# A two-layer transformer decoder on one Trainium2 core: the cross-attention softmax handed on by four heads instead of eight

## The chip, the core and the metric

The kernel runs on one core of one Trainium2 chip. A core has five engines, each with its own instruction queue that is worked off strictly in order: TensorE (PE in the profile, with its weight loads as PEld), VectorE (DVE), ScalarE (ACT), GpSimd (POOL) and SyncE (SP, which here only issues transfers). They meet through semaphores. The metric is device time in microseconds of one execution. Three executions of the kernel before took 549.65, 549.88 and 549.92 us, median 549.88 us.

## The reference, cut to what matters

Sixteen sequences of 128 tokens with 128 features pass through six residual blocks, each behind a layer norm:

```python
x = x + attn0(ln(x))            # self0: 16 heads of 8, causal
x = x + xattn0(ln(x), ctx)      # cross0: 8 heads of 64
x = x + ternary_ffn(ln(x))      # ffn
x = x + attn1(ln(x))            # self1: 16 heads of 8, causal, scores clipped
x = x + xattn1(ln(x), ctx)      # cross1: 16 heads of 64
x = x + mixture(ln(x))          # moe: 8 experts, gated
```

The part at issue is the softmax of the two cross attentions. For each head, with 128 queries on the partitions and 128 keys along the row:

```python
attn = softmax(scores, axis=-1)   # max, exp(scores - max), sum, division
out  = attn @ v
```

## The kernel before

The program is a stream of small steps. A step has a name such as `cross1.rc.1` (stage, step, chunk), and each exists once per sequence. A chunk is eight heads (`UNIT` = 8), so that one chunk's scores are a tile of 128 x 1024 float32 in one of two PSUM groups `S`. cross0 has one chunk per sequence and cross1 two, which makes 3 x 16 = 48 chunks of cross softmax. In this text `@7` behind a step's name is the sequence.

What one chunk of cross softmax does, step by step:

- `s1` (PE, `cross_scores1`, line 986; matmuls at L995): eight score tiles into a group of S.
- `mx` (DVE, `negative_max`, L769): one reduction over 128 x 1024 to eight negated maxima.
- `ex` (ACT, `cross_exps`, L649): eight exponentials of 128 x 128, from S to `diff` (also called `e`) in SBUF. The last one frees the group of S.
- `rc` (DVE, `reciprocal_sums`, L776 to L778): one reduction over 128 x 1024 to eight sums, a drain, eight reciprocals.
- `nz` (POOL, `divide_by_sum`, L577): one multiplication over 128 x 1024, in place.
- `t` (PE, `turn_over`, L1008): eight transposes into a group of S.
- `wT` (ACT, `weights_by_key`, L658) copies them to SBUF, and `pv` (PE, L1035) multiplies with the values.

self0 also has a `t` step, with the same helper and line; its input is made by `self0.mx` on DVE (`less_max`, L785 and L787: maximum, drain, subtraction, each over 128 x 1024, for two chunks per sequence). Its transposes are named `diff_self` in the trace, those of the cross stages `diff_cross`.

The order of all steps on each engine is settled before the program is written. The class `Plan` (line 199) places steps by estimated weights and by the priorities in the table `FORWARD`, and runs up to a dozen sequences in different stages beside each other. `run` (line 483) then writes each engine's steps out in that order. So an engine that waits at one step holds back all that is behind it. A step's waits and semaphore counts are written out in its helper, and the two groups of S and the four banks X are shared by all stages in the planned turn.

Of the kernel before, what the change touches and what calls it, by code (L numbers as in the profile page):

```python
# [9 lines left out]
ALU = mybir.AluOpType  # L10
ACT = mybir.ActivationFunctionType
AX_X = mybir.AxisListType.X

P = 128
# [3 lines left out]
UNIT = 8  # L18
# [16 lines left out]
class Step:  # L35
# [280 lines left out]
class CrossAttention(Attention):  # L316
    def __init__(self, nc, ctx, name, heads):
        Attention.__init__(self, nc, ctx, name, heads, heads // UNIT, XD, heads // UNIT, True)
        self.v = [self.sb(f"v{b}", [P, heads, XD]) for b in range(AHEAD[name])]
        self.kT = [self.sb(f"kT{b}", [P, heads // 2, P]) for b in range(AHEAD[name])]  # L320
        self.qT = self.sb("qT", [P, heads // 2, P])
        self.e = self.diff
        self.e_sum = self.sb("e_sum", [P, self.units, UNIT])
        self.e_rec = self.sb("e_rec", [P, self.units, UNIT])
        self.max_ready = [self.sem(f"max_ready{u}") for u in range(self.units)]
        self.rec_ready = [self.sem(f"rec_ready{u}") for u in range(self.units)]


def halves(ap):
# [4 lines left out]
def v_halves(v):  # L334

    return v[:].rearrange("p h s w -> p (h s w)").bitcast(BF16).rearrange(
        "p (h s w two) -> p h s w two", s=3, w=SD + 1, two=2)[:, :, :, :, 1]


def place(head):  # L340

    return 4 * (head % 2) + head % UNIT // 2


def decoder(nc, t, out):
    ctx = ExitStack()
    with ctx:
# [3 lines left out]
        def sem(name):  # L351
            return ctx.enter_context(nc.semaphore(name))
# [4 lines left out]
        x_full, s_full = sem("x_full"), sem("s_full")  # L357
# [13 lines left out]
        def score(i, *names):  # L371

            return max(scored[i, n] for n in names)
# [54 lines left out]
        self0 = SelfAttention(nc, ctx, "self0", True)  # L428
# [83 lines left out]
        def _(pool):  # L512
# [60 lines left out]
                    .then_inc(L.low_ready[u], 1)  # L573

            def divide_by_sum(L, i, u):
                pool.wait_ge(L.rec_ready[u], i + 1)
                pool.tensor_tensor(L.diff[u][:].rearrange("p (h k) -> p h k", h=UNIT),  # L577
                                   L.e[u][:].rearrange("p (h k) -> p h k", h=UNIT),
                                   L.e_rec[:, u, :].unsqueeze(2).broadcast_to([P, UNIT, P]), ALU.mult)\
                    .then_inc(L.diff_ready[u], 1)  # L580

            def mix_experts(i):
                pool.wait_ge(*taken(i, "moe.e"))
# [27 lines left out]
        def _(act):  # L611
# [29 lines left out]
            def cross_exps(L, i, u):  # L641

                turn = f"{L.name}.s1.{u}"
                S_ = group(i, turn)
                act.wait_ge(L.max_ready[u], i + 1)
                if i:
                    act.wait_ge(s_full, score(i - 1, f"{L.name}.t.{u}"))
                for p in range(UNIT):
                    last = act.activation(L.e[u][:, P * p:P * (p + 1)], S_[:, P * p:P * (p + 1)], ACT.Exp,  # L649
                                          bias=L.row_max[:, u, p:p + 1])  # L650
                last.then_inc(taken(i, turn)[0], 1)

            def weights_by_key(L, i, u):
# [19 lines left out]
            def do_step(i, name, L, step, u):  # L673
# [39 lines left out]
                if step == "ex" and L in (cross0, cross1):  # L713
                    cross_exps(L, i, u)
# [24 lines left out]
        def _(dve):  # L739
# [26 lines left out]
            def negative_max(L, i, u):  # L766
                turn = f"{L.name}.s1.{u}"
                dve.wait_ge(s_full, score(i, turn))
                dve.tensor_reduce(L.row_max[:, u, :], group(i, turn)[:].rearrange("p (h k) -> p h k", h=UNIT), AX_X,  # L769
                                  ALU.max, negate=True).then_inc(L.max_ready[u], 1)  # L770

            def reciprocal_sums(L, i, u):
                dve.wait_ge(*taken(i, f"{L.name}.s1.{u}"))
                if i:
                    dve.wait_ge(L.diff_ready[u], i)
                dve.tensor_reduce(L.e_sum[:, u, :], L.e[u][:].rearrange("p (h k) -> p h k", h=UNIT), AX_X, ALU.add)  # L776
                dve.drain()
                dve.reciprocal(L.e_rec[:, u, :], L.e_sum[:, u, :]).then_inc(L.rec_ready[u], 1)  # L778

            def less_max(L, i, u):  # L780
                scores = group(i, f"{L.name}.s1", u)[:].rearrange("p (h k) -> p h k", h=UNIT)
# [111 lines left out]
            def do_step(i, name, L, step, u):  # L893
# [44 lines left out]
        def _(pe):  # L938
# [5 lines left out]
            def room_for_scores(i, name, turns=1):  # L944
                for k in range(turns):
                    if plan.turn[i, name, k][0]:
                        pe.wait_ge(s_free[plan.bank[i, name, k]], plan.turn[i, name, k][0])
# [38 lines left out]
            def cross_scores1(L, i, name, c):  # L986
                pe.wait_ge(*emptied(i, f"{L.name}.q.{c}"))
                pe.wait_ge(*emptied(i, f"{L.name}.k.{c}"))
                if i:
                    pe.wait_ge(L.diff_ready[c], i)  # L990
                room_for_scores(i, name)
                S_, kT = group(i, name), L.kT[i % AHEAD[L.name]]
                for h in range(UNIT * c, UNIT * (c + 1)):
                    rows, at = slice(XD * (h % 2), XD * (h % 2 + 1)), P * place(h)
                    last = pe.matmul(S_[:, at:at + P], L.qT[rows, h // 2, :],  # L995
                                     kT[rows, h // 2, :],
                                     start=True, stop=True)
                last.then_inc(s_full, 1)

            def turn_over(L, i, name, u):  # L1000
                if L is self0:
                    S_ = group(i, f"{L.name}.s1", u)
                else:
                    S_ = group(i, name)
                    room_for_scores(i, name)
                pe.wait_ge(L.diff_ready[u], i + 1)
                for k in range(UNIT):
                    last = pe.transpose(S_[:, P * k:P * (k + 1)], L.diff[u][:, P * k:P * (k + 1)], ident[:])  # L1008
                last.then_inc(s_full, 1)

# [199 lines left out]
```

## Time and profile before

| | |
|---|---|
| median of three executions | 549.88 us |
| the profiled execution itself | 549.28 us |
| span of its trace | 547.5 us |
| PE / ACT / DVE / POOL busy | 516.0 / 436.6 / 400.7 / 383.2 us |
| instructions | 15960 |

The span goes from the first to the last instruction of the program; the execution's own time also holds 1.8 us around it. Busy time of an engine is the time in which at least one of its instructions was at work. Matmuls overlap one another and their ends are modelled, so for PE the starts of matmuls say more than the busy time.

### The profile page before, as it was taken

The page shows a single profiled execution, that of the slowest core. Times are in us where ns is not written, and L with a number is a line of the kernel's source. Part 1 is how long each engine was busy: PE and PEld are TensorE (multiplying, and loading weights), DVE is VectorE, ACT ScalarE, POOL GpSimd, SP SyncE. Part 2 cuts the span into 40 slices and gives each one's busy share as a digit, 9 for nine tenths or more (in the row PEclk, how much of TensorE's full clock was granted, in tenths as well). Part 3 has the DMA queues.
Part 4 walks back from the last instruction along what each step waited for, and adds up shares of the span by engine and source line. Part 5 has one row for each costly group of instructions (what it writes and reads, how often), then busy time and mean ns, then how long its engine had stood idle before and what let it go on. Part 6 is the DMA issues. An engine that isn't in the chain of part 4 may idle for free.

```text
span 547.5 us, 15960 instructions
## 1 busy us (share of the span) xinstructions
PE 516.0 (94%) x5506; PEld 414.3 (76%) x5506; DVE 400.7 (73%) x904; ACT 436.6 (80%) x1154; POOL 383.2 (70%) x566
## 2 busy tenths in 40 slices
PE   4999979899999999999999999999999999999974
PEld 3778657687788888887887978878788877777851
DVE  1655857786879798888878797978887758665553
ACT  3678775889789897998888888989888886898641
POOL 5356547877687879787778788776886756575454
PEclk9999998999999999999999999999999999999987
DMA  6800000000000000000000000000000000000000
GB/s 198 306 2 2 1 1 2 1 3 2 2 1 8 2 7 3 6 2 8 2 6 2 8 1 2 7 2 8 1 7 1 2 6 8 1 6 2 7 6 10
DMA packets 6462, 8.95 MB, mean 16 GB/s; under 512 B 1008, under 2 KB 4848, under 8 KB 6384
## 3 DMA queue, kind: packets, MB, share of 16 engines
q1 hardware_dynamic: 6384, 7.94, 4.4%
q8 instruction: 45, 0.74, 0.6%
q14 instruction: 33, 0.27, 0.2%
HBM read 6.50 MB, written 1.05 MB: 14 GB/s over the span
## 4 chain that ended last, share of the span: by engine, by line
PE 72%; issue 7%; POOL 6%; ACT 5%; POOLq 5%; DVE 4%; DVEq 2%; ACTq 0%
PE X L952 14%; PE S L1008 10%; PE S L995 8%; PE X L1044 8%; PE X L1035 7%; PE X L1092 6%; PE S L982 5%; PE S L1128 3%; POOL w_low_self L572 3%; ACT diff_cross L649 3%; PE X L1055 2%; PE X L1146 2%; PE X L1021 2%; POOL diff_cross L577 2%; POOLq L544 1%
## 5 line engine op out<-in xcount | busy, mean ns | idle before, releaser
L572 POOL TENSOR_TENSOR w_low_self<-w_self 128x1024 f16<-128x1024 f32 x64 | 120.5, 1893 | 47.8 <-ACT w_self L638 32.0
L649 ACT ACTIVATE diff_cross<-S,row_max_cross 128x128 f32<-128x128 f32 x384 | 103.7, 408 | 5.3 <-DVE row_max_cross L769 5.1
L577 POOL TENSOR_TENSOR diff_cross<-diff_cross,e_rec_cross 128x1024 f32<-128x1024 f32 x48 | 91.0, 1897 | 17.4 <-DVE e_rec_cross L778 17.2
L769 DVE TENSOR_REDUCE row_max_cross<-S 128x8 f32<-128x1024 f32 x48 | 58.4, 1218 | 28.7 <-PE S L995 28.6
L776 DVE TENSOR_REDUCE e_sum_cross<-diff_cross 128x8 f32<-128x1024 f32 x48 | 58.3, 1215 | 9.9 <-ACT diff_cross L649 9.9
L658 ACT ACTIVATE w_cross<-S 128x1024 f32<-128x1024 f32 x48 | 50.0, 1048 | 6.5 <-PE S L1008 6.1
L1008 PE MATMUL S<-ident,diff_cross 128*128 128x128 f32 x384 | 49.7, 274 | 5.2 <-POOL diff_cross L577 3.1
L995 PE MATMUL S<-kT_cross,qT_cross 64*128 64x128 f32 x768 | 52.6, 281 | 2.2 <-ACT qT_cross L614 1.1
L1008 PEld LDWEIGHTS S<-ident,diff_cross 128*128 128x128 f32 x384 | 42.9, 141 | 12.8 <-issue 4.4
L796 DVE SCALAR_TENSOR_TENSOR w_self<-S,s_bound 128x1024 f32<-128x1024 f32 x32 | 37.6, 1216 | 19.2 <-PE S L982 19.2
L995 PEld LDWEIGHTS S<-kT_cross,qT_cross 64*128 64x128 f32 x768 | 45.7, 187 | 7.7 <-issue 4.5
L1035 PEld LDWEIGHTS X<-w_cross,v_cross 128*64 128x64 f32 x768 | 41.6, 138 | 13.0 <-issue 7.4
L1035 PE MATMUL X<-w_cross,v_cross 128*64 128x128 f32 x768 | 51.1, 279 | 0.2 <-issue 0.2
L614 ACT ACTIVATE attnT_cross<-X 128x512 f32<-128x512 f32 x48 | 28.7, 601 | 22.1 <-PE X L1035 21.7
L785 DVE TENSOR_REDUCE row_max_self<-S 128x8 f32<-128x1024 f32 x32 | 38.9, 1217 | 3.7 <-PE S L982 3.6
L787 DVE TENSOR_TENSOR diff_self<-S,row_max_self 128x1024 f32<-128x1024 f32 x32 | 39.2, 1225 | 2.4
L982 PE MATMUL S<-by_head_self,plain_self 32*128 32x512 f32 x256 | 37.8, 661 | 1.4 <-ACT diff_cross L649 1.3
L638 ACT ACTIVATE w_self<-S 128x1024 f32<-128x1024 f32 x32 | 33.2, 1036 | 6.6 <-PE S L1008 6.6
L614 ACT ACTIVATE qT_cross<-X 128x512 f32<-128x512 f32 x48 | 28.7, 599 | 11.2 <-PE X L952 11.1
L614 ACT ACTIVATE by_head_self<-X,head_mask 128x128 f32<-128x128 f32 x128 | 36.4, 378 | 0.0
L614 ACT ACTIVATE kT_cross<-X 128x512 f32<-128x512 f32 x48 | 29.8, 622 | 7.6 <-PE X L952 7.6
L1008 PE MATMUL S<-ident,diff_self 128*128 128x128 f32 x256 | 33.7, 275 | 1.9 <-DVE diff_self L787 1.7
(156 smaller groups left out, 1299.1 us busy)
## 6 DMA issues: line engine op xcount, KB each, us to landing
out_dram<-x_all SPq DMA_DIRECT2D x16, 64.0 KB, 1.5
x_all<-in_x SPq DMA_DIRECT2D x1, 768.0 KB, 6.9
cT_all<-in_ctx SPq DMA_DIRECT2D x1, 768.0 KB, 8.8
e_k<-in_e_k SPq DMA_DIRECT2D x1, 512.0 KB, 4.5
e_v<-in_e_v SPq DMA_DIRECT2D x1, 512.0 KB, 5.5
e_q<-in_e_q SPq DMA_DIRECT2D x1, 512.0 KB, 8.6
e_o<-in_e_o SPq DMA_DIRECT2D x1, 512.0 KB, 10.5
m_w<-in_m_w SPq DMA_DIRECT2D x1, 512.0 KB, 8.8
```

Source lines behind the costliest of these rows:

```text
L572: pool.tensor_tensor(L.w_low[u][:], L.w[u][:], halves(L.w[u][:]), ALU.subtract)\
L577: pool.tensor_tensor(L.diff[u][:].rearrange("p (h k) -> p h k", h=UNIT), L.e[u][:].rearrange("p (h k) -> p h k", h=UNIT), L.e_rec[:, u, :] ...
L614: act.activation(dst, src, ACT.Copy, **scale).then_inc(emptied(i, name)[0], 1)
L649: last = act.activation(L.e[u][:, P * p:P * (p + 1)], S_[:, P * p:P * (p + 1)], ACT.Exp, bias=L.row_max[:, u, p:p + 1])
L658: act.activation(L.w[u][:], group(i, turn)[:], ACT.Copy).then_inc(taken(i, turn)[0], 1)
L769: dve.tensor_reduce(L.row_max[:, u, :], group(i, turn)[:].rearrange("p (h k) -> p h k", h=UNIT), AX_X, ALU.max, negate=True).then_inc(L.ma ...
L776: dve.tensor_reduce(L.e_sum[:, u, :], L.e[u][:].rearrange("p (h k) -> p h k", h=UNIT), AX_X, ALU.add)
L952: last = pe.matmul(bank(i, name)[:, P * k:P * (k + 1)], w[:, col:col + P], xT, start=True, stop=True)
L982: last = pe.matmul(group(i, name, u)[:, 512 * half:512 * (half + 1)], L.plain[rows, :], L.by_head[rows, :, :].rearrange("p j n -> p (j n)" ...
L995: last = pe.matmul(S_[:, at:at + P], L.qT[rows, h // 2, :], kT[rows, h // 2, :], start=True, stop=True)
L1008: last = pe.transpose(S_[:, P * k:P * (k + 1)], L.diff[u][:, P * k:P * (k + 1)], ident[:])
L1035: last = pe.matmul(bank(i, name)[rows, P * pair:P * (pair + 1)], v[:, h, :], L.w[c][:, P * place(h):P * (place(h) + 1)], start=True, stop= ...
```

## The change

The planned steps, their order and their weights stay as they are. Inside the steps `mx`, `ex`, `rc` and `nz` of the cross stages, each chunk is worked in two pieces of four heads, and each piece is announced by itself. `row_max`, `e_sum`, `e_rec` and `e` are the same tensors. The semaphores `max_ready`, `rec_ready` and `diff_ready` of the cross stages now count two per chunk and sequence, and a new one, `exp_half`, is raised by the fourth exponential. The group of S is still freed by the eighth. The transposes of a cross chunk wait for the first piece before the first and for the second before the fifth.

```diff
+def pieces(i):
+    return [(slice(0, 4), 1), (slice(4, 8), 1)]
+
+def columns(ap, heads):
+    return ap[:, P * heads.start:P * heads.stop].rearrange("p (h k) -> p h k", k=P)
...
             def divide_by_sum(L, i, u):
-                pool.wait_ge(L.rec_ready[u], i + 1)
-                pool.tensor_tensor(L.diff[u][:]..., L.e[u][:]..., L.e_rec[:, u, :]..., ALU.mult)\
-                    .then_inc(L.diff_ready[u], 1)
+                for heads, n in pieces(i):
+                    pool.wait_ge(L.rec_ready[u], 2 * i + heads.stop // 4)
+                    pool.tensor_tensor(columns(L.diff[u], heads), columns(L.e[u], heads), ..., ALU.mult)\
+                        .then_inc(L.diff_ready[u], n)
...
             def cross_exps(L, i, u):
-                act.wait_ge(L.max_ready[u], i + 1)
-                if i:
-                    act.wait_ge(s_full, score(i - 1, f"{L.name}.t.{u}"))
-                for p in range(UNIT):
-                    last = act.activation(L.e[u][:, P * p:P * (p + 1)], ...)
+                for heads, n in pieces(i):
+                    act.wait_ge(L.max_ready[u], 2 * i + heads.stop // 4)
+                    if i and heads.start == 0:
+                        act.wait_ge(s_full, score(i - 1, f"{L.name}.t.{u}"))
+                    for p in range(heads.start, heads.stop):
+                        last = act.activation(L.e[u][:, P * p:P * (p + 1)], ...)
+                    if heads.stop == 4:
+                        last.then_inc(L.exp_half[u], 1)
                 last.then_inc(taken(i, turn)[0], 1)
...
             def negative_max(L, i, u):
                 dve.wait_ge(s_full, score(i, turn))
-                dve.tensor_reduce(L.row_max[:, u, :], ..., ALU.max, negate=True).then_inc(L.max_ready[u], 1)
+                for heads, n in pieces(i):
+                    dve.tensor_reduce(L.row_max[:, u, heads], columns(group(i, turn), heads), ...)\
+                        .then_inc(L.max_ready[u], n)
...
             def reciprocal_sums(L, i, u):
-                dve.wait_ge(*taken(i, f"{L.name}.s1.{u}"))
-                ...
-                dve.tensor_reduce(L.e_sum[:, u, :], ..., ALU.add)
-                dve.drain()
-                dve.reciprocal(L.e_rec[:, u, :], L.e_sum[:, u, :]).then_inc(L.rec_ready[u], 1)
+                for heads, n in pieces(i):
+                    if heads.stop == 4:
+                        dve.wait_ge(L.exp_half[u], i + 1)
+                    else:
+                        dve.wait_ge(*taken(i, f"{L.name}.s1.{u}"))
+                    if i and heads.start == 0:
+                        dve.wait_ge(L.diff_ready[u], 2 * i)
+                    dve.tensor_reduce(L.e_sum[:, u, heads], columns(L.e[u], heads), AX_X, ALU.add)
+                    dve.drain()
+                    dve.reciprocal(L.e_rec[:, u, heads], L.e_sum[:, u, heads]).then_inc(L.rec_ready[u], n)
...
             def turn_over(L, i, name, u):
                 if L is self0:
                     S_ = group(i, f"{L.name}.s1", u)
+                    pe.wait_ge(L.diff_ready[u], i + 1)
                 else:
                     S_ = group(i, name)
                     room_for_scores(i, name)
-                pe.wait_ge(L.diff_ready[u], i + 1)
                 for k in range(UNIT):
+                    if L is not self0 and (k == 4 or k == 0):
+                        pe.wait_ge(L.diff_ready[u], 2 * i + 1 + k // 4)
                     last = pe.transpose(S_[:, P * k:P * (k + 1)], L.diff[u][:, P * k:P * (k + 1)], ident[:])
```

## Rows read from the trace of the kernel before

**Rows 1.** Windows: busy us (instructions) of PE, PEld, DVE, ACT, POOL; clock; DMA.

```profile
20.00:150.00 130.00, 121.30 (x1305) 94.87 (x1304) 90.94 (x188) 102.06 (x262) 83.41 (x122) 0.99 0.05 16
150.00:440.00 290.00, 289.40 (x3272) 238.80 (x3272) 237.71 (x532) 253.02 (x676) 229.00 (x322) 1.00 0.02 4
440.00:547.50 107.50, 92.85 (x848) 71.16 (x846) 63.84 (x168) 71.50 (x193) 61.95 (x88) 0.96 0.02 5
```

**Rows 2.** Groups: line, tiles, count | busy us, mean ns | idle before us, its releaser.

```profile
L649 ACT ACTIVATE diff_cross<-S,row_max_cross 128x128 f32<-128x128 f32 x384 | 103.7, 408 | 5.3 <-DVE row_max_cross L769 5.1
L577 POOL TENSOR_TENSOR diff_cross<-diff_cross,e_rec_cross 128x1024 f32<-128x1024 f32 x48 | 91.0, 1897 | 17.4 <-DVE e_rec_cross L778 17.2
L776 DVE TENSOR_REDUCE e_sum_cross<-diff_cross 128x8 f32<-128x1024 f32 x48 | 58.3, 1215 | 9.9 <-ACT diff_cross L649 9.9
L1008 PE MATMUL S<-ident,diff_cross 128*128 128x128 f32 x384 | 49.7, 274 | 5.2 <-POOL diff_cross L577 3.1 <-ACT w_cross L658 1.1 <-ACT diff_cross L649 0.7
```

**Rows 3.** Groups with shorter rows of the same kinds of instruction, same columns.

```profile
L808 DVE TENSOR_REDUCE o_sum_self<-X 128x144 f32<-128x432 f32 x32 | 19.2, 600 | 4.4 <-PE X L1023 4.4
L586 POOL TENSOR_TENSOR weighted<-weighted 128x512 f32<-128x512 f32 x16 | 20.3, 1269 | 6.6 <-DVE weighted L865 6.6
L588 POOL TENSOR_TENSOR weighted<-weighted 128x256 f32<-128x256 f32 x16 | 11.6, 728 | 2.3
```

**Rows 4.** Timeline of DVE: start, us, what, [idle before, releaser].

```profile
312.81 0.29 DVE L828 TENSOR_TENSOR x_all<-X,x_all 128x128 f32<-128x128 f32 x1 [0.21 <-PE X L1044]
...
315.36 1.22 DVE L776 TENSOR_REDUCE e_sum_cross<-diff_cross 128x8 f32<-128x1024 f32 x1
...
321.70 1.23 DVE L787 TENSOR_TENSOR diff_self<-S,row_max_self 128x1024 f32<-128x1024 f32 x1
...
325.37 1.21 DVE L769 TENSOR_REDUCE row_max_cross<-S 128x8 f32<-128x1024 f32 x1
326.50 0.15 DVE L843 RECIPROCAL g_rec<-g_sum 128x1 f32<-128x1 f32 x1
```

**Rows 5.** Timeline of PE in the same stretch (sequence 12), same columns.

```profile
322.98 1.09 PE L1008 MATMUL S<-ident,diff_self 128*128 128x128 f32 x8
```

**Rows 6.** Timeline, DVE and PE: the same pair in sequences 7 and 14.

```profile
174.34 1.23 DVE L787 TENSOR_TENSOR diff_self<-S,row_max_self 128x1024 f32<-128x1024 f32 x1
175.62 1.09 PE L1008 MATMUL S<-ident,diff_self 128*128 128x128 f32 x8
...
382.01 1.23 DVE L787 TENSOR_TENSOR diff_self<-S,row_max_self 128x1024 f32<-128x1024 f32 x1
383.29 0.33 PE L1008 MATMUL S<-ident,diff_self 128*128 128x128 f32 x1
```

**Rows 7.** Timelines of DVE and PE: sequence 13, with two sums ahead of it.

```profile
346.38 1.21 DVE L776 TENSOR_REDUCE e_sum_cross<-diff_cross 128x8 f32<-128x1024 f32 x1
347.79 1.20 DVE L776 TENSOR_REDUCE e_sum_cross<-diff_cross 128x8 f32<-128x1024 f32 x1
...
353.02 1.22 DVE L787 TENSOR_TENSOR diff_self<-S,row_max_self 128x1024 f32<-128x1024 f32 x1
354.49 0.38 PE L1008 MATMUL S<-ident,diff_self 128*128 128x128 f32 x2
```

**Rows 8.** Timelines: where PE waits for the cross softmax (start, sequences 2 and 14).

```profile
42.33 0.44 PE L967 MATMUL S<-mask,ident_b 32*32 32x512 bf16 x16 [0.39 <-ACT diff_cross L649]
80.17 1.90 POOL L577 TENSOR_TENSOR diff_cross<-diff_cross,e_rec_cross 128x1024 f32<-128x1024 f32 x1
82.22 0.95 PE L1008 MATMUL S<-ident,diff_cross 128*128 128x128 f32 x7 [1.73 <-POOL diff_cross L577]
503.10 1.21 DVE L776 TENSOR_REDUCE e_sum_cross<-diff_cross 128x8 f32<-128x1024 f32 x1
504.67 1.90 POOL L577 TENSOR_TENSOR diff_cross<-diff_cross,e_rec_cross 128x1024 f32<-128x1024 f32 x1 [5.30 <-DVE e_rec_cross L778]
506.71 0.96 PE L1008 MATMUL S<-ident,diff_cross 128*128 128x128 f32 x7 [0.85 <-POOL diff_cross L577]
```

More of the change, by code:

```diff
@@ L326, in __init__ @@
         self.rec_ready = [self.sem(f"rec_ready{u}") for u in range(self.units)]
+        self.exp_half = [self.sem(f"exp_half{u}") for u in range(self.units)]
 def halves(ap):
@@ L575, in divide_by_sum @@
             def divide_by_sum(L, i, u):
-                pool.wait_ge(L.rec_ready[u], i + 1)
-                pool.tensor_tensor(L.diff[u][:].rearrange("p (h k) -> p h k", h=UNIT),
-                                   L.e[u][:].rearrange("p (h k) -> p h k", h=UNIT),
-                                   L.e_rec[:, u, :].unsqueeze(2).broadcast_to([P, UNIT, P]), ALU.mult)\
-                    .then_inc(L.diff_ready[u], 1)
+                for heads, n in pieces(i):
+                    pool.wait_ge(L.rec_ready[u], 2 * i + heads.stop // 4)
+                    pool.tensor_tensor(columns(L.diff[u], heads), columns(L.e[u], heads),
+                                       L.e_rec[:, u, heads].unsqueeze(2).broadcast_to([P, 4 * n, P]), ALU.mult)\
+                        .then_inc(L.diff_ready[u], n)
             def mix_experts(i):
@@ L644, in cross_exps @@
                 S_ = group(i, turn)
-                act.wait_ge(L.max_ready[u], i + 1)
-                if i:
-                    act.wait_ge(s_full, score(i - 1, f"{L.name}.t.{u}"))
-                for p in range(UNIT):
-                    last = act.activation(L.e[u][:, P * p:P * (p + 1)], S_[:, P * p:P * (p + 1)], ACT.Exp,
-                                          bias=L.row_max[:, u, p:p + 1])
+                for heads, n in pieces(i):
[3 more added lines that the diff above has]
+                    for p in range(heads.start, heads.stop):
+                        last = act.activation(L.e[u][:, P * p:P * (p + 1)], S_[:, P * p:P * (p + 1)], ACT.Exp,
+                                              bias=L.row_max[:, u, p:p + 1])
+                    if heads.stop == 4:
+                        last.then_inc(L.exp_half[u], 1)
                 last.then_inc(taken(i, turn)[0], 1)
@@ L768, in negative_max @@
                 dve.wait_ge(s_full, score(i, turn))
-                dve.tensor_reduce(L.row_max[:, u, :], group(i, turn)[:].rearrange("p (h k) -> p h k", h=UNIT), AX_X,
-                                  ALU.max, negate=True).then_inc(L.max_ready[u], 1)
+                for heads, n in pieces(i):
+                    dve.tensor_reduce(L.row_max[:, u, heads], columns(group(i, turn), heads), AX_X,
+                                      ALU.max, negate=True).then_inc(L.max_ready[u], n)
             def reciprocal_sums(L, i, u):
-                dve.wait_ge(*taken(i, f"{L.name}.s1.{u}"))
-                if i:
-                    dve.wait_ge(L.diff_ready[u], i)
-                dve.tensor_reduce(L.e_sum[:, u, :], L.e[u][:].rearrange("p (h k) -> p h k", h=UNIT), AX_X, ALU.add)
-                dve.drain()
-                dve.reciprocal(L.e_rec[:, u, :], L.e_sum[:, u, :]).then_inc(L.rec_ready[u], 1)
+                for heads, n in pieces(i):
[8 more added lines that the diff above has]
+                    dve.reciprocal(L.e_rec[:, u, heads], L.e_sum[:, u, heads]).then_inc(L.rec_ready[u], n)
             def less_max(L, i, u):
@@ L989, in cross_scores1 @@
                 if i:
-                    pe.wait_ge(L.diff_ready[c], i)
+                    pe.wait_ge(L.diff_ready[c], 2 * i)
                 room_for_scores(i, name)
```

## Prediction

> **What bounds the kernel now.** I first read the busy time of each engine by stretch [rows 1]. From 150 to 440 us PE is busy 289.40 of 290.00 us, with DVE at 82%, ACT at 87% and POOL at 79%: in the middle PE bounds, and nearly every delay put into PE's queue lengthens the kernel by as much. Up to 150 us PE sits idle for 8.70 of 130 us and after 440 us for 14.65 of 107.5 us; there, chains of waits matter and a shorter softmax could pay.
>
> Next come the groups, for what each engine of the cross softmax waits for before its step [rows 2]. The reader is to see how little idle time the softmax's own latency causes. ACT is idle before its 384 exponentials for 5.3 us in all. PE is idle before the 384 cross transposes for 3.1 us because of POOL. The plan puts `t` late enough that the chain of mx, ex, rc and nz is long finished in the middle.
>
> Then the timeline, for what PE does wait for in the middle. DVE works without a pause from 312.81 us, released by PE's `cross1.y`, until well past 326 us, and on this run stand in this order: three residuals, `cross1.rc.1`, `self1.at`, `self0.mx.0`, `self0.mx.1` [rows 4]. The last subtraction ends at 321.70 + 1.23 = 322.93 us, and PE's `self0.t.1` starts at 322.98 [rows 5]: it is just in time, with 0.05 us for the semaphore. The first and the last sequence with this pattern show the same 0.05 us: 175.57 to 175.62 and 383.24 to 383.29 us [rows 6]. Six sequences have it with one cross sum ahead in the run (7, 8, 9, 10, 12, 14). So the resource with no slack is DVE's run ahead of self0's transposes, and the change makes just that run longer.
>
> **The change part by part.**
>
> *DVE, maxima.* A reduction over 1024 occupies DVE from 325.37 to 326.50, 1.13 us [rows 4]. The slope comes from 432 against 1024 elements: (1.215 - 0.600) / 592 = 1.04 ns each, 1.064 us for 1024 [rows 2, 3]. Two halves cost one fixed part more: 1.13 - 1.06 = 0.07 us. The upper bound is the whole fixed part of the duration, 1.215 - 1.064 = 0.15 us, if the halves did not overlap.
>
> *DVE, sums.* A step `rc` takes 1.41 us start to start, 346.38 to 347.79 [rows 7]. Split, its reduction's fixed part, the drain and the reciprocals come twice: 1.41 - 1.06 = 0.35 us more. Lower bound: 0.12 us, should the second reduction hide all but the reciprocals' issue. Upper bound: 0.50 us, with the 0.15 us above for a wait between the halves. I take 0.35, since nothing after a drain overlaps in these rows. Where the step now waits for `ex` (9.9 us of idle in all, [rows 2]), the first half is hidden in that wait and `rc` ends about 0.5 us earlier instead. In sum 48 x (0.07 + 0.35) = 20 us of DVE work.
>
> The next instruction starts at 326.50, 0.08 us before the reduction ends at 325.37 + 1.21 = 326.58 [rows 4]. The Trainium skill, "VectorE: DVE Perf Modes", section "The DRAIN you can't avoid", says that the next operation does not start before the pipe is empty; by that rule the split maxima would cost the upper 0.15 us and each run below 0.1 to 0.2 us more. The trace does not bear it out.
>
> *POOL.* From 512 and 256 elements, 1.269 and 0.728 us, a slope of 2.11 ns and a fixed part of 0.19 us [rows 3]. A half of the division is then (1.897 - 0.19) / 2 + 0.19 = 1.04 us, the pair 0.19 us longer (bounds 0, if fixed parts overlap, and 0.19); 48 x 0.19 = 9 us. In the middle POOL has 61 of 290 us idle [rows 1], three divisions per sequence of 29 us make 0.6 us, and no step of PE there is released by POOL within that: I take nothing.
>
> *ACT.* The exponentials stay as they are, with one more wait and increment in their midst: between 0 and 48 x 0.05 us (the semaphore's time above) = 2.4 us; I take 0, as ACT would only stop there if DVE's second half were late, and that takes 0.7 us against four exponentials of 103.7 / 384 = 0.27 us each [rows 2], 1.1 us. Starting earlier pays only where ACT is idle before the first one: 5.1 us, mostly at the start [rows 2].
>
> *PE.* No instruction more; one more wait in the middle of each cross `t`. When PE arrives the semaphore is mostly set; bounds 0 and 48 x 0.05 = 2.4 us, and I take 0.
>
> *What PE loses in the middle.* Each sum ahead of `self0.t.1` in an unbroken run delays it by 0.35 us. Split maxima ahead of `cross1.res` are covered by the 0.21 us of idle before 312.81 [rows 4]. Six sequences x 0.35 = 2.1 us. Sequences 6 and 13 have both chunks' sums and maxima in the run, 2 x 0.42 = 0.84 us; 13 has 354.49 - 354.24 = 0.25 us in hand, of which the semaphore takes 0.05 [rows 7], so it loses 0.64, and 6, which is tight, 0.8. Sequences 11 and 15 have looser ends; I put 0.3 and 0.2 us. Sum 4.0 us. Behind PE stand all later steps, and DVE's run starts from PE's `cross1.y` again, so these delays add up over the sequences and aren't made good; a tenth I let go for waits on other engines: 3.6 us.
>
> *What PE gains at the ends.* At 42.33 PE waits 0.39 us for the group of S that `cross0.ex.0@0` frees, and ACT stood idle before it: 0.4 us. At 82.22 it waited 1.73 us for POOL; that division starts at 80.17 with no idle time before it, so POOL came from other work and had its sums already [rows 8]; two halves end 0.2 us later than one, and only the transposes of the first half move up: 0.2 us. In sequence 14 sum, division and transposes follow each other directly [rows 8]: the first division can start at 503.10 + 0.7 + 0.3 = 504.1 instead of 504.67, the second ends at 506.2 to 506.4, and only four transposes are then left: 0.5 us; sequence 13 has 0.2 us in the same way. Sum 1.3 us. The last sequence's end is made by the experts' steps, which don't change.
>
> **The sum.** The profiled execution took 549.28 us: 549.28 + 3.6 - 1.3 = 551.6 us. That execution was 0.6 us under the median of the three runs, 549.88; moved there, 552.2 us, 0.4% slower.
>
> **The rivals.**
>
> *The delays are swallowed.* PE isn't quite full: 0.60 us of idle in the middle by these windows, and starts that lie further apart than they need. If PE's delay at `self0.t.1` only replaces waits it would have had later for ACT, the loss falls to about 1.3 us and the ends pay it back. For it: ACT and DVE are both above 80%. Against: the run is released by PE itself. Time: 549.9 us.
>
> *The shorter chain wins, on the other side.* Place: the transposes of the cross stages, and the start of the exponentials. Per chunk the time from scores to transposes shrinks by half a reduction twice (1.1 us) and half a division (0.9 us), less the fixed parts. Price: the 3.1 us of PE's waits before cross transposes plus the 0.4 us at the start go [rows 2, 8], and DVE's 20 us find room in the 290 - 237.7 = 52 us it has idle in the middle. It decides if the added 0.35 us is less than what the run gains at its head, that is if `rc` stands where DVE waits. For it: POOL idles 17.2 us on the reciprocals. Against: these are the ends, and before `self0.mx` DVE has no pause. Time: 549.9 - 3.5 = 546.4 us. The Trainium skill, "Perfetto Trace Analysis", section "Optimizing Scalar/DVE Operations", gives a rule for this side: where an unsaturated engine makes bubbles on another, cutting its instructions up can finish work sooner. In this trace the bubbles are few.
>
> *The small delays breed.* The upper prices (0.50 + 0.15 us per chunk) make each run 0.6 us longer, and further steps with little in hand behind them (the experts' weights, `cross1.t.1`) come late too: 4.0 x 0.6 / 0.35 = 6.9 us, less 1.3 and with 1 us for those steps, 556.5 us.
>
> **How the numbers follow.** Forecast 0.46, swallowed 0.24, shorter chain 0.17, breeding 0.13. The time is the forecast's, 552.2 us; its own range is 551.0 to 554.0. For 8 in 10 the range takes in the swallowed case whole and part of the other two: 548.8 to 556.0. A difference of under 0.2% (1.1 us) is about what can't be told from no change. Slower by more: forecast and breeding, 0.59; within: 0.24; faster: 0.17.
>
> **What would show it.** In the profile after, DVE should be busy some 20 us more, and reductions over 512 should take about 0.68 us each; POOL some 8 us more. The timeline should show `self0.t.1` of sequences 7 to 14 starting 0.05 us after a later DVE, with PE idle before it and DVE named as its releaser, and PE's idle in the middle up by 2 to 4 us. Before the cross transposes POOL's name should shrink below 3.1 us. I am wrong if a split `rc` costs under 0.2 us, if DVE's run ahead of `self0.mx` starts earlier relative to PE, or if the ends gain more than 3 us.

## The result: 0.26% slower, and the profile after

Median 550.67 us for the changed kernel beside 549.49 us for the kernel before in the same comparison: ratio 1.0026, 95% interval 1.0016 to 1.0035, which is 0.9 to 1.9 us more. The prediction said 552.2 us and "slower by more than 0.2%" with 0.59. Its sign holds. Its time is 1.5 us too high: 0.4 us of that is the kernel before, which came out at 549.49 us here instead of 549.88, and the rest is the size of the change, forecast at 2.3 us and measured at 1.4 us by the ratio (1.2 us by the medians). That the change is past 0.2% (1.1 us) hangs on the point value; the interval begins at 0.9 us. The profiled execution took 550.7 us with a span of 549.0 us and 16200 instructions.

Windows of the kernel after; columns as in [rows 1], which they answer:

```profile
20.00:150.00 130.00, 121.61 (x1295) 94.83 (x1294) 92.69 (x212) 101.23 (x261) 83.78 (x130) 0.97 0.05 17
150.00:440.00 290.00, 288.85 (x3250) 236.88 (x3247) 244.04 (x620) 251.56 (x671) 231.57 (x349) 1.00 0.02 4
440.00:549.00 109.00, 94.59 (x880) 73.04 (x878) 67.69 (x200) 74.04 (x199) 65.08 (x101) 0.98 0.02 6
```

PE stays full in the middle; DVE is busy there for 6.3 us more than before (244.04 against 237.71). Groups of the page after, to set beside [rows 2]: line, tiles, count, then busy and mean, then idle before and releaser.

```profile
L660 ACT ACTIVATE diff_cross<-S,row_max_cross 128x128 f32<-128x128 f32 x384 | 103.7, 410 | 2.8 <-DVE row_max_cross L783 2.6
L588 POOL TENSOR_TENSOR diff_cross<-diff_cross,e_rec_cross 128x512 f32<-128x512 f32 x96 | 97.7, 1039 | 8.8 <-DVE e_rec_cross L796 8.8
L783 DVE TENSOR_REDUCE row_max_cross<-S 128x4 f32<-128x512 f32 x96 | 61.4, 682 | 28.5 <-PE S L1013 28.4
L794 DVE TENSOR_REDUCE e_sum_cross<-diff_cross 128x4 f32<-128x512 f32 x96 | 64.2, 669 | 2.9 <-ACT diff_cross L660 2.2 <-issue 0.3
...
L1028 PE MATMUL S<-ident,diff_cross 128*128 128x128 f32 x384 | 50.0, 274 | 3.8 <-ACT diff_cross L660 1.2 <-POOL diff_cross L588 1.2 <-ACT w_cross L671 1.1
...
L1028 PE MATMUL S<-ident,diff_self 128*128 128x128 f32 x256 | 34.2, 277 | 2.7 <-DVE diff_self L805 2.3
```

Everything that a shorter chain should shorten did get shorter: ACT's idle time before the exponentials fell from 5.3 to 2.8 us, POOL's before the divisions from 17.4 to 8.8, DVE's before the sums from 9.9 to 2.9, PE's on POOL from 3.1 to 1.2 us. The kernel is slower all the same. What pays for it is in DVE's run; here is the run of sequence 12 in the trace after, the counterpart of [rows 4, 5] (start, us, what, and in brackets the idle time before, which is printed from 0.15 us on):

```profile
314.70 0.29 DVE L846 TENSOR_TENSOR x_all<-X,x_all 128x128 f32<-128x128 f32 x1
...
317.25 0.69 DVE L794 TENSOR_REDUCE e_sum_cross<-diff_cross 128x4 f32<-128x512 f32 x1
318.00 0.18 DVE L796 RECIPROCAL e_rec_cross<-e_sum_cross 128x4 f32<-128x4 f32 x1
318.10 0.65 DVE L794 TENSOR_REDUCE e_sum_cross<-diff_cross 128x4 f32<-128x512 f32 x1
318.83 0.18 DVE L796 RECIPROCAL e_rec_cross<-e_sum_cross 128x4 f32<-128x4 f32 x1
318.93 0.61 DVE L826 TENSOR_REDUCE o_sum_self<-X 128x144 f32<-128x432 f32 x1
...
323.87 1.23 DVE L805 TENSOR_TENSOR diff_self<-S,row_max_self 128x1024 f32<-128x1024 f32 x1
```

The run is released by PE as before. In both traces the residual starts 0.31 us after the last matmul of `cross1.y` (312.50 and 314.39 us); DVE is idle ahead of it for 0.21 us before and 0.14 us after, since the chunk's split maxima ahead of it take 0.07 us of that. PE in the same stretch:

```profile
322.08 0.61 PE L1075 MATMUL X<-xnT_self,d_qk 128*128 128x128 f32 x4
322.72 1.09 PE L1028 MATMUL S<-ident,diff_self 128*128 128x128 f32 x8
...
324.65 0.61 PE L1075 MATMUL X<-xnT_self,a_qk 128*128 128x128 f32 x4
325.15 1.09 PE L1028 MATMUL S<-ident,diff_self 128*128 128x128 f32 x8
```

The sum takes 318.93 - 317.25 = 1.68 us now. From the residual that PE's `cross1.y` releases to `self0.t.1` it is 325.15 - 314.70 = 10.45 us, where [rows 4, 5] have 322.98 - 312.81 = 10.17. That is 0.28 us more, and PE still starts 325.15 - (323.87 + 1.23) = 0.05 us behind DVE. The transposes have no idle bracket: PE's wait hides in the modelled end of the matmul before. Starts show it. Here are the same two PE instructions ahead of `self0.t.0` in the kernel before:

```profile
320.19 0.61 PE L1055 MATMUL X<-xnT_self,d_qk 128*128 128x128 f32 x4
320.64 1.04 PE L1008 MATMUL S<-ident,diff_self 128*128 128x128 f32 x8
```

0.45 us from start to start before, 0.64 after, and the group's mean rose from 275 to 277 ns instead of its idle time.

So from here on I read each trace by starts of PE's steps against those of the kernel before. All kernels have the same 5506 matmuls in the same order, so they can be set side by side one by one. The table's "middle" is how much such a shift grows between `cross1.y` of sequence 0 (134.5 us before) and of sequence 10 (430.0 us); at 1.00 granted clock in all of them. "Clock" is the granted clock in the windows 80 to 90 and 520 to 530 us.

| kernel | time against before, us (95%) | middle, us | clock 80:90, 520:530 |
|---|---|---|---|
| before | | | 0.83, 0.83 |
| after | +1.4 (0.9 to 1.9) | +2.57 | 0.67, 1.00 |
| after, once more | +1.4 (0.4 to 2.4) | +2.64 | 0.66, 0.83 |
| only sums split | +2.7 (1.9 to 3.6) | +3.19 | 0.67, 0.86 |
| only division split | -0.5 (-1.5 to 0.4) | +0.22 | 0.83, 0.83 |
| only maxima split | -1.0 (-1.8 to -0.2) | -0.60 | 0.83, 0.83 |
| all split, only at the ends | -1.8 (-2.7 to -0.8) | -0.14 | 0.66, 1.00 |
| all split, 13 sums in the run whole | -1.7 (-2.6 to -0.8) | +0.11 | 0.83, 0.83 |
| dose in the run, 0.285 us x 10 | +1.9 (0.9 to 2.9) | +2.15 | 0.66, 0.83 |
| same dose off the run | -0.4 (-1.3 to 0.5) | 0.00 | 0.73, 1.00 |
| double dose in the run, 0.611 us x 10 | +5.3 (4.2 to 6.3) | +5.12 | 0.72, 0.91 |
| ends, and maxima everywhere | -1.4 (-2.5 to -0.3) | -0.22 | 0.83, 0.83 |
| 13 sums whole, division at the ends | -1.3 (-2.5 to 0.0) | +0.06 | 0.66, 0.83 |

The times are the ratios of each comparison times 549.9 us. A ratio is not the quotient of the two medians: the medians differ by 3.4 us for "only sums split", 2.0 for "after, once more", 0.0 for "only division split" and +0.3 for "same dose off the run". All of these lie in their intervals, so single tenths of a microsecond in this column mean nothing.

### The profile page after: what moved, and what is told of

Read it like the earlier page. It is cut to its first block, busy times and chain, and to the rows that moved or that the text cites. A ratio compares the mean times of both kernels' runs of the same rounds, so it can differ in the third digit from the quotient of the medians.

```text
span 549.0 us, 16200 instructions
## 1 busy us (share of the span) xinstructions
PE 517.5 (94%) x5506; PEld 414.3 (75%) x5506; DVE 412.5 (75%) x1048; ACT 437.2 (80%) x1154; POOL 389.7 (71%) x614
## 4 chain that ended last, share of the span: by engine, by line
PE 71%; DVE 6%; issue 6%; ACT 5%; POOLq 4%; POOL 4%; DVEq 4%; ACTq 0%
PE X L970 13%; PE S L1028 10%; PE S L1013 8%; PE X L1055 7%; PE X L1064 7%; PE X L1112 6%; PE S L1000 4%; PE S L1148 4%; ACT diff_cross L660 3%; POOL w_low_self L582 2%; PE X L1075 2%; PE X L1166 2%; DVEq L804 2%; PE X L1041 2%; POOLq L554 1%
## 5 line engine op out<-in xcount | busy, mean ns | idle before, releaser
L588 POOL TENSOR_TENSOR diff_cross<-diff_cross,e_rec_cross 128x512 f32<-128x512 f32 x96 | 97.7, 1039 | 8.8 <-DVE e_rec_cross L796 8.8
L783 DVE TENSOR_REDUCE row_max_cross<-S 128x4 f32<-128x512 f32 x96 | 61.4, 682 | 28.5 <-PE S L1013 28.4
L794 DVE TENSOR_REDUCE e_sum_cross<-diff_cross 128x4 f32<-128x512 f32 x96 | 64.2, 669 | 2.9 <-ACT diff_cross L660 2.2
L642 ACT ACTIVATE w_self<-w_self,shift 128x1024 f32<-128x1024 f32 x32 | 35.5, 1140 | 0.0
```

The costliest lines, as they stand in the source:

```text
L588: pool.tensor_tensor(columns(L.diff[u], heads), columns(L.e[u], heads), L.e_rec[:, u, heads].unsqueeze(2).broadcast_to([P, 4 * n, P]), ALU ...
L783: dve.tensor_reduce(L.row_max[:, u, heads], columns(group(i, turn), heads), AX_X, ALU.max, negate=True).then_inc(L.max_ready[u], n)
L794: dve.tensor_reduce(L.e_sum[:, u, heads], columns(L.e[u], heads), AX_X, ALU.add)
```

## The experiments

All kernels come from the changed one by three switches, which say for each stage, sequence and chunk whether a part is split; with all three on it is the changed kernel, with all off the kernel before.

```diff
-def pieces(i):
-    return [(slice(0, 4), 1), (slice(4, 8), 1)]
+HALVES = [slice(0, 4), slice(4, 8)]
+def parts(split, L, i, u):     # split is max_split, sum_split or div_split
+    return HALVES if split(L.name, i, u) else [slice(0, 8)]
...
-                for heads, n in pieces(i):
+                for heads in parts(sum_split, L, i, u):
```

**Which part of the change costs.** Only the sums:

```diff
 def max_split(L, i, u):
-    return True
+    return False
 def div_split(L, i, u):
-    return True
+    return False
```

> Only the sums and reciprocals are split, all sixteen sequences; maxima and division are whole, and the division waits for both halves. Theory: self0.t loses 0.3 us in each of the sequences 7 to 14, 2.5 to 3 us in all as with the whole change, and little is gained at the ends since the division is not handed on: 551.5 to 552.5 us. Rival 1 (the loss comes from the maxima or from POOL's halves): 549.5 us, self0.t unmoved. Rival 2 (the second half's latency is hidden in the pipe and the loss is PE's additional waits): 549.5 to 550 us.

Measured: +2.7 us (median 553.31 us), so at or above the top of what I expected. It looks worse than the whole change, but the intervals overlap. Sequence 12 in its trace:

```profile
315.10 0.29 DVE L871 TENSOR_TENSOR x_all<-X,x_all 128x128 f32<-128x128 f32 x1 [0.21 <-PE X L1090]
...
317.01 0.18 DVE L783 BATCH_NORM_AGGREGATE mean_var_cross<-moments_cross 128x2 f32<-128x6 f32 x1 [0.42 <-issue]
...
317.99 0.69 DVE L819 TENSOR_REDUCE e_sum_cross<-diff_cross 128x4 f32<-128x512 f32 x1
...
324.62 1.23 DVE L830 TENSOR_TENSOR diff_self<-S,row_max_self 128x1024 f32<-128x1024 f32 x1
```

```profile
323.47 1.09 PE L1054 MATMUL S<-ident,diff_self 128*128 128x128 f32 x8 [0.17 <-DVE diff_self L830]
325.90 1.09 PE L1054 MATMUL S<-ident,diff_self 128*128 128x128 f32 x8
```

The run is again released by PE's `cross1.y` with 0.21 us of idle, as in [rows 4], and PE follows its end by 0.05 us. The split sums alone make a loss in the middle as large as that of the whole change. That it is 3.19 us and not 2.6 has another cause. From residual to `self0.t.1` it is 325.90 - 315.10 = 10.80 us here, 0.35 more than the 10.45 above, and the row at 317.01 shows why: DVE stands still for 0.42 us and waits for nothing that the profile shows. Such stops are in every trace and fall on other instructions when DVE's queue holds more or fewer of them (see the last section). In this trace sequences 9 and 12 lose 0.61 and 0.69 us, where each has one split sum of 0.27 us.

Only the division (`div_split` true, the others false):

> Only the division on POOL is split, with the transposes' waits; sums and maxima are whole. Theory: DVE's run ahead of self0.mx is as before, so no loss in the middle; the first four transposes of a chunk can start 1 us after the division's start at the ends: 548.5 to 549.3 us. Rival 1 (POOL's added 6.5 us of work or PE's added waits cost in the middle, up to 48 x 0.05 us): 550 to 552 us. Rival 2 (nothing at the ends comes from the division): 549.5 us.

Measured: -0.5 us, an interval that holds zero. My range of 548.5 to 549.3 us was missed by the median (549.93), and the second rival (nothing gained at the ends) fits as well. POOL's longer pairs and PE's added waits cost nothing that can be told. Only the maxima:

> Only the maxima are split, in all sixteen sequences; sums and division are whole. Theory: 0.07 us per chunk more for DVE, most of it hidden at the head of the run by cross1.res's wait for PE, and the exponentials can start 0.5 us earlier where ACT waits: 549 to 550 us, no difference that can be told. Rival 1 (any added instruction in DVE's queue costs): 0.6 us x 10 sequences of run and a start 0.15 us later each, 551.5 us. Rival 2 (the ends' gain of 1.8 us comes from the exponentials' earlier start): 548 us.

Measured: -1.0 us, 0.2 to 1.8 faster, which lies between the theory and its second rival: part of the ends' gain is the exponentials' earlier start. The 0.46 us at PE's group of S at 42.33 [rows 8] is gained. The middle gives 0.60 us, but 0.38 of it comes in one step, in sequence 10, and no wait of the softmax goes away there. In the kernel before, one of DVE's stops falls into that sequence's run; with the maxima split it falls elsewhere. First the kernel before, then the one with split maxima:

```profile
257.18 0.60 DVE L808 TENSOR_REDUCE o_sum_self<-X 128x144 f32<-128x432 f32 x1
258.22 0.26 DVE L812 RECIPROCAL X<-o_sum_self 128x16 f32<-128x16 f32 x1 [0.44 <-issue]
```

```profile
257.01 0.59 DVE L851 TENSOR_REDUCE o_sum_self<-X 128x144 f32<-128x432 f32 x1
257.68 0.26 DVE L855 RECIPROCAL X<-o_sum_self 128x16 f32<-128x16 f32 x1
```

The three parts add up within the noise: in the middle 3.19 + 0.22 - 0.60 = 2.81 beside 2.57 and 2.64 for the whole; in time 2.7 - 0.5 - 1.0 = 1.2 beside 1.4 us. As the stops fall differently in each, that they agree to 0.2 us is partly luck.

**Where it costs.** Everything split, but 13 of 48 sums left whole, those in the run:

```diff
 def sum_split(L, i, u):
-    return True
+    return not (L == "cross1" and u == 1 and 1 <= i <= 10) and not (L == "cross1" and i in (1, 8, 10))
```

> Everything is split but the sums that stand in DVE's run ahead of self0.mx: cross1's second chunk of sequences 1 to 10 and its first of 1, 8 and 10 have whole sums (13 of 48). Their maxima and divisions are still split. Theory: the loss of self0.t in sequences 6 to 15 falls from about 3 us to under 0.6 us, the ends' gain stays: 547.8 to 548.8 us, faster than both kernels. Rival (any added DVE work costs, wherever it stands): 35 of 48 sums still split, 550.4 us. Rival (the split maxima ahead in the run cost as well): 549.5 to 550 us.

Measured: -1.7 us, and the middle shifts by 0.11 us instead of 2.6. The median, 548.48 us, lies in the range expected. With 35 of 48 sums still split, the loss is gone. In its trace, sequence 12:

```profile
314.52 1.22 DVE L819 TENSOR_REDUCE e_sum_cross<-diff_cross 128x8 f32<-128x1024 f32 x1
...
320.87 1.23 DVE L830 TENSOR_TENSOR diff_self<-S,row_max_self 128x1024 f32<-128x1024 f32 x1
...
322.85 0.69 DVE L819 TENSOR_REDUCE e_sum_cross<-diff_cross 128x4 f32<-128x512 f32 x1
```

The sum ahead of `self0.mx` is whole, the one behind it is split. Splitting only at the two ends:

```diff
 def sum_split(L, i, u):          # max_split and div_split alike
-    return True
+    return (i <= 2 or i >= 12) if L == "cross0" else (i == 0 or i >= 11)
```

> Maxima, sums and division are split only at the two ends: cross0 of sequences 0 to 2 and 12 to 15, cross1 of sequences 0 and 11 to 15; all other chunks run as before the change. Theory (the middle loses because a split sum is 0.3 us longer ahead of self0.mx in DVE's unbroken run, the ends gain): the middle is as before, the ends keep what they gave, 0.6 us without the granted clock and up to 1.8 us with it, so 547.7 to 548.9 us. Rival 1 (any added DVE work costs): a third of the split chunks costs a third of 1.2 us, 549.9 us. Rival 2 (the gain at the end was the granted clock alone and not the change): 549.3 to 549.7 us, with self0.t of sequences 7 to 12 where they were before.

Measured: -1.8 us, 548.1 us, as expected, so the ends gain by themselves. The second rival, that this gain is granted clock, is answered by the executions with the same mean clock. At 0.989 this kernel has a median of 548.10 us (8 executions) and the kernel before 549.69 (14 in the same comparison), 1.6 us more; the kernel that spares the run has 548.59 us (8). In the second comparison of the changed kernel ("once more") it has 551.29 us at 0.989 and the kernel before 549.93 (8 each), so its loss isn't clock either.

**Is it DVE's time, and nothing of the hand-over?** The kernel before, with work that nobody uses (and one fill of `idle_in` on POOL at the start):

```diff
                     dve.reciprocal(L.e_rec[:, u, heads], L.e_sum[:, u, heads]).then_inc(L.rec_ready[u], 1)
+                if L.name == "cross1" and u == 1 and 1 <= i <= 10:
+                    dve.tensor_reduce(idle_out[:], idle_in[:].rearrange("p (a b) -> p a b", a=2), AX_X, ALU.max)
```

> The kernel before, with one idle reduction over 2x128 numbers (about 0.33 us of DVE, its result used by nobody) right behind the reciprocals of cross1's second chunk in sequences 1 to 10, so ten of them ahead of self0.mx of sequences 6 to 15. Nothing is split. Theory: each delays self0.t by its own duration, so 0.2 to 0.33 us in each sequence, 2.3 to 3.3 us in all, 552 to 553 us. Rival (the loss comes of the hand-over in halves, its waits and latencies, and not of DVE's time): 549.5 to 550 us.

Measured: +1.9 us. That is under the 2.3 to 3.3 us expected; of this range the interval (0.9 to 2.9) holds the lower part. One dose, in its timeline of DVE:

```profile
315.91 0.29 DVE L876 TENSOR_TENSOR x_all<-X,x_all 128x128 f32<-128x128 f32 x1 [0.20 <-PE X L1095]
...
319.75 0.20 DVE L824 RECIPROCAL e_rec_cross<-e_sum_cross 128x8 f32<-128x8 f32 x1
319.87 0.37 DVE L826 TENSOR_REDUCE idle_out<-idle_in 128x2 f32<-128x256 f32 x1
...
325.08 1.23 DVE L835 TENSOR_TENSOR diff_self<-S,row_max_self 128x1024 f32<-128x1024 f32 x1
```

```profile
326.37 1.09 PE L1059 MATMUL S<-ident,diff_self 128*128 128x128 f32 x8
```

The row says 0.37 us, but it overlaps its neighbours: by start to start it takes 0.285 us, and the stretch from residual to `self0.t.1` is 326.37 - 315.91 = 10.46 us, the same 10.45 as with the split sum. Ten doses of 0.285 put in 2.85 us, and 2.15 us come out in the middle, with no hand-over split. The sequences 13 and 15 pass on nothing, as their runs have something in hand; the other eight pass on 2.15 of 2.28 us. The same dose elsewhere (`L.name == "cross0" and 3 <= i <= 12`):

> The kernel before, with the same idle reduction, ten of them, behind the reciprocals of cross0's one chunk in sequences 3 to 12, which stands outside the run ahead of self0.mx but for sequences 13 and 15. Nothing is split. Theory: DVE has idle time there (52 of 290 us in the middle), so 549.5 to 550.2 us. Rival (any DVE time costs, wherever it stands): the same 552 to 553 us as with the reductions behind cross1's sums.

Measured: -0.4 us, an interval that holds zero, and a middle of 0.00 us. Two of the ten doses lie ahead of the measured stretch, at 102 and 129 us; nine of the ten have a wait of DVE of 0.65 us or more behind them before the next `self0` subtraction, which takes them up. The same DVE work costs 1.9 us in one place and nothing that can be told in the other. And twice the dose in the run (a second such line):

> The kernel before, with two of the idle reductions at each of the ten places behind cross1's second sum (0.6 us each time). Theory: the delay grows in step with the time put in, so twice the loss of the single one: 4.7 to 6.5 us, 554.3 to 556.2 us. Rival (later waits give it back, or other steps break too): under 1.3 times or over 2.5 times the loss of the single one.

Measured: +5.3 us, middle +5.12 us for 6.11 us put in (start to start, the second of each pair takes 0.326 us). That is 2.4 times the single dose in the middle and 2.8 times in the time, which is above "twice", and by the time also above the 2.5 times that the rival named for other steps breaking too. The intervals of both are wide enough for twice, and the trace decides: sequences 13 and 15, which passed on nothing of the single dose, now pass on 0.31 and 0.09 us, and the other eight 4.6 of 4.9 us, the same 0.95 of what is put in as with the single dose. So what slack there was is used up, and nothing further breaks. The theory's 554.3 to 556.2 us holds the median, 555.53; that later waits would give the delay back does not hold.

**Once more, and a better version.**

> The changed kernel once more (all three split in all sixteen sequences), beside the same runs of the kernel before as the two that follow. Theory: a ratio as the first time, 1.0016 to 1.0035, so 0.9 to 1.9 us slower. If it comes out within 0.1% of the kernel before, the loss read from the traces (2.6 us in the middle, less the ends' gain) is a matter of single executions.

Measured: +1.4 us, as the first time. For the next two kernels the switches above are mixed: maxima split everywhere, division at the ends, and the sums at the ends or everywhere but in the run.

> Maxima split in all sixteen sequences, sums and division only at the two ends (as in the kernel split only there). Theory: the ends' gain (1.7 us) and what the split maxima gave in the middle when they were split alone (0.6 us) come together: 2.3 us under the kernel before, 0.4 to 0.7 us under the kernel split only at the ends. Rival (the 0.6 us in the middle was the phase of one execution): no better than 1.8 us under the kernel before.

> Maxima split everywhere, sums split everywhere but in DVE's run ahead of self0.mx (13 of 48 whole), division split only at the ends. Theory: sums outside the run and halves of the division in the middle neither cost nor give, so the same as with both at the ends alone, 1.7 to 2.3 us under the kernel before. Rival (POOL's divided divisions in the middle cost a little, each 0.19 us): 0.3 to 0.6 us faster than the kernel that spared only the run, so 2.0 to 2.3 us under. Rival (the split sums cost outside the run too): 1.5 us under or less.

Measured: -1.4 and -1.3 us. Neither shows itself better than the kernel split only at the ends (its -1.8 us lies in both intervals, and the first one's middle is -0.22 us, not -0.60). The first kernel's expected 2.3 us didn't come; its rival, no more than 1.8 us, did. For the second, the time alone would also fit the rival that split sums cost outside the run too (1.5 us or less), but its middle of +0.06 us, where the sums outside the run are split, speaks against it. Sequence 10 gives 0.36 us in both, as with the maxima alone, but the first loses 0.26 again in sequence 11. So the 0.60 us is mostly a matter of where DVE's stops fall, and not of an earlier start. The kernel split at the ends and the one that spares the run beat both the kernel before and the changed one (548.1 and 548.48 us beside 549.95 in the same comparison; the changed one was 1.4 us above the kernel before in its own two); the simpler is the one split at the ends.

## Why the prediction was right, and where its sizes were off

*The place* was right, and is shown: DVE's run ahead of `self0.mx`, released by PE and followed by PE at 0.05 us. Sparing it takes the loss away, a dose in it brings the loss back, and the same dose outside costs nothing that can be told.

*The price of a split sum* was put at 0.35 us with bounds 0.12 and 0.50. It is 1.68 - 1.41 = 0.27 us, and the median over 43 steps without a pause is 1.68 us too. One more row of the kernel before, between the two sums of [rows 7]:

```profile
347.67 0.20 DVE L778 RECIPROCAL e_rec_cross<-e_sum_cross 128x8 f32<-128x8 f32 x1
```

Start to start, the reduction with its drain took 347.67 - 346.38 = 1.29 us and the reciprocals 0.12; the halves take 0.75 and 0.73, and 0.10 each. The forecast kept the reciprocals' 0.12 us whole for each half, which is 0.04 us too much. It reckoned each half reduction at 1.29 - 0.53 = 0.76 us by a slope taken from another shape, which is 0.04 us too much for the two. "Nothing after a drain overlaps" was misread, since the next sum started 0.08 us before the reciprocals' end in the kernel before as well (347.79 against 347.87). It didn't make the price wrong: the 1.41 us, start to start, already held that overlap. The maxima cost 0.07 us a step, as said (1.21 instead of 1.14 us).

*The loss in the middle* was put at 3.6 us and measured 2.6. By sequence, the shift of `self0.t.1` grew by 0.51, 0.28, 0.31, -0.09, 0.34 and 0.21 us in the sequences 7, 8, 9, 10, 12 and 14, 1.56 us where 6 x 0.35 = 2.1 was forecast; by 0.20 in sequence 6 (0.8 forecast), 0.32 in 13 (0.64), 0.20 in 11 (0.3) and 0.28 in 15 (0.2). With 0.27 instead of 0.35 us for each sum the same working gives 1.62 + 0.68 + 0.48 + 0.5 = 3.3 us, and a tenth less, 2.9 us. So the mis-sized term is the sum's price. Of the rest, sequence 6 lost 0.2 instead of 0.7 us; why its two sums did not both count stays open. Sequence 10 lost its 0.27 us like the others and won back 0.36 us, because the stop of 0.44 us at 258.22 no longer fell into its run. That part is luck, which no term of the forecast held.

*The gain at the ends* was put at 1.3 us. Rows of the trace after, against [rows 8]:

```profile
80.68 0.63 PE L1028 MATMUL S<-ident,diff_cross 128*128 128x128 f32 x4 [0.88 <-POOL diff_cross L588]
81.59 0.66 PE L1028 MATMUL S<-ident,diff_cross 128*128 128x128 f32 x4 [0.28 <-POOL diff_cross L588]
...
507.13 2.04 POOL L588 TENSOR_TENSOR diff_cross<-diff_cross,e_rec_cross 128x512 f32<-128x512 f32 x2 [4.88 <-DVE e_rec_cross L796]
509.38 1.09 PE L1028 MATMUL S<-ident,diff_cross 128*128 128x128 f32 x8 [0.51 <-ACT diff_cross L660]
```

At 42.33 PE's 0.39 us of waiting is gone and its steps move up by 0.46 us (0.4 forecast). At 82.22 the wait falls from 1.73 to 0.88 + 0.28 us and the transposes start 0.86 us earlier, but within two steps, at `ffn.y`, 0.8 us of it is lost again: 0.05 instead of 0.2 us. In sequence 14 the wait falls from 0.85 to 0.51 us, gaining 0.33 instead of 0.5, since `cross1.t` now waits for ACT's group of S and no longer for POOL: a new wait in the place of the old. In sequence 13 it gains 0.63 us (0.2 forecast), half of it lost just ahead at `self1.oT` (0.34). Together 0.46 + 0.05 + 0.33 + 0.63 - 0.34 = 1.1 us. The sum by these measured terms, 2.6 - 1.1 = 1.5 us, is the 1.4 us that the comparison shows. The two kernels that keep the ends and spare the run are 1.7 and 1.8 us faster than before, with a middle of about nothing; that is more than 1.1 us, though 1.1 lies in both intervals. Both terms of the forecast were too large, so the errors (1.0 and 0.2 us) partly cancelled.

*POOL, ACT and PE.* POOL's pair takes 2.04 instead of 1.90 us, 0.14 for the 0.19 said, and was rightly taken at nothing. DVE's busy time rose by 412.5 - 400.7 = 11.8 us, not 20. Start to start it is 48 x (0.07 + 0.27) = 16 us; the idle time of 0.07 us between each sum's reduction and its reciprocals, in the drain, comes 48 times more and is no busy time, which makes 3.5 us of the difference.

*What would show it* was half wrong. I expected PE idle before `self0.t`, named as released by DVE and 2 to 4 us more. It is 2.3 instead of 1.7 us, and PE's idle in all of the middle rose from 0.60 to 1.15 us; the rest of the wait stands in the lengthened interval since PE's step before.

*Of the rivals*, the swallowed delays are out: a dose came out at 0.75 to 0.84 of its size. The breeding is out: 0.611 us at once bred nothing beyond itself. The shorter chain is right about the ends and wrong about the whole, and it has its point of decision: take the sums out of the run and it wins by 1.7 us. The Trainium skill, "Perfetto Trace Analysis", section "Optimizing Scalar/DVE Operations", says that cutting an unsaturated engine's instructions up can end work sooner by removing another engine's bubbles. These runs agree where PE waits for the chain (the ends: 1.7 us). Where there is no such bubble the rule promises nothing, and the runs show the price: the cut piece stands in an in-order queue ahead of something due. The Trainium skill, "VectorE: DVE Perf Modes", section "The DRAIN you can't avoid", says that the next operation does not start until the pipe is empty, and adds: "A next op that is not held starts earlier". The prediction left this out. In the trace after, the reduction at 318.10 starts before the reciprocal that began at 318.00 and takes 0.18 has ended, so these rows go with the addition. They don't show what "held" means there.

## What to carry to other kernels

Before a step of a full pipeline is cut in two, look at what is queued behind it on its own engine: the fixed part of the second piece (here 0.27 us for reduction, drain and reciprocals) is paid by whatever stands behind with no slack, and it is paid every round when the run begins with a release by the bounding engine. Cut where an engine waits, and leave whole what stands ahead of a step that is just in time. An idle instruction of known length put into a queue measures the slack of a place for the price of one run. And an added instruction can also move stops of its engine onto other instructions, so a shift is read at several places before it is put down to the edit.

## What the runs showed of the hardware

The granted clock fell at 80 to 90 us and after 520 us in all or most traces, and in three also at 110 to 120 us (0.83). The first two are stretches where PE is not full (7 to 8 of 10 us busy), and the fall was not equally long each time. Windows of the kernel before and, last, of the kernel with the dose off the run; columns as in [rows 1]:

```profile
80.00:90.00 10.00, 7.23 (x90) 4.57 (x90) 6.93 (x14) 4.79 (x7) 9.09 (x15) 0.83 0.01 2
520.00:530.00 10.00, 7.31 (x46) 4.99 (x48) 5.97 (x18) 4.97 (x16) 7.39 (x9) 0.83 0.01 2
```

```profile
520.00:530.00 10.00, 6.91 (x53) 4.81 (x53) 6.69 (x21) 6.43 (x21) 6.10 (x7) 1.00 0.01 2
```

Granted 0.83 and 1.00 is a mixture of the levels of 1.2 and 2.4 GHz in the one and the upper level throughout in the other. One step of PE, the experts' matmuls of sequence 13, in the kernel before and in the kernel after:

```profile
522.07 3.37 PE L1128 MATMUL S<-m_w,moe_xnT 128*128 128x512 f32 x4
```

```profile
524.57 1.96 PE L1148 MATMUL S<-m_w,moe_xnT 128*128 128x512 f32 x4
```

1.41 us, as much as the whole change costs, and it also appears with the dose off the run, whose end isn't changed at all: the same step takes 1.96 us there. At 80 to 90 us the window has 0.83 in five traces and 0.66 to 0.73 in the other eight. From `self0.t.0` of sequence 3 to that of sequence 4 the shift against the kernel before changes by -0.12 to +0.06 us in the first kind and by +0.55 to +1.08 us in the second, whatever the edit. What decides which level a stretch gets stayed open. Single profiled executions of these kernels can therefore differ by 1 us and, with both places together (0.96 + 1.41), by 2.4 us for nothing that was edited: time is compared over many executions, and traces are compared stretch by stretch.

DVE now and then stands still for 0.2 to 0.5 us in the midst of its work, where the profile names nothing that it waits for (`issue`). Two of these stops, at 258.22 in the kernel before and at 317.01 with only the sums split, are shown above. The kernel before has eight of over 0.2 us in its trace; in the order of DVE's recorded instructions they are about 75 apart or a multiple of that (74, 75, 146, 147, 149). The two traces of the changed kernel have ten each, on the very same instructions:

```profile
306.81 0.21 DVE L766 TENSOR_SCALAR y_scale<-a_scale,t_scale 128x1 f32<-128x1 f32 x1 [0.43 <-issue]
```

```profile
307.76 0.21 DVE L791 TENSOR_SCALAR y_scale<-a_scale,t_scale 128x1 f32<-128x1 f32 x1 [0.43 <-issue]
```

So their place goes with the number of instructions in the queue and not with the execution. Where one falls into a run without slack it costs PE about 0.36 us (10.54 us from residual to `self0.t.1` in sequence 10 before, 10.17 in sequence 12). What makes them stayed open.
